# Expert blocks of 256 rows in place of 384, and the second weight split once by GpSimd during plain attention

## The reference

```python
x = x + attention_1(layernorm(x))          # 16 heads, relative positions clipped at 64
# second layer
h = layernorm(x)
q, k, v = split(h @ w_qkv + b_qkv)         # 16 heads of 16
x = x + attention(q, k, v) @ w_o + b_o     # plain attention
h = layernorm(x)
logits = h @ gate_w + gate_b
topv, topi = top_k(logits, 2)              # 2 of 8 experts per token
ew = scatter of softmax(topv)
hid = relu(h @ W1[e] + b1[e])              # 256 -> 1024
x = x + sum over the 2 experts of ew * (hid @ W2[e] + b2[e])   # 1024 -> 256
```

## Time and profile before

| | |
|---|---|
| median of 3 runs | 4359.0 us (4358.93 to 4363.57) |
| span of the profiled execution, first to last instruction | 4340.7 us, 18.3 below that median |
| mean granted clock of TensorE over the span | 0.951 of full speed |
| busy over the span: TensorE, VectorE, ScalarE, GpSimd | 91%, 80%, 69%, 33% |
| DMA: bytes, mean rate | 556 MB, 128 GB/s |

### The profile page before, as it was taken

One profiled execution on the slowest core, in us unless ns is written; L12 is line 12 of the kernel. 1 busy time (PEld: TensorE's weight loads), 2 busy tenths in 40 slices (PEclk: granted clock), 3 DMA queues, 4 the chain that ended last, 5 costly groups with the idle time before them and its releaser, 6 DMA issues. The chain is left out here.

```text
span 4340.7 us, 77253 instructions
## 1 busy us (share of the span) xinstructions
PE 3962.5 (91%) x26592; PEld 2108.1 (49%) x26592; DVE 3486.0 (80%) x6304; ACT 2981.4 (69%) x5821; POOL 1446.1 (33%) x1405
## 2 busy tenths in 40 slices
PE   8699999999999999996799999999999996599997
PEld 5355555555455555544433333333333333499997
DVE  6788888888888888835688898888888872477775
ACT  4078888888788878881148888888888883266664
POOL 0356666666666666641100000000000001522232
PEclk9599999999999999998879999999999997699998
DMA  8566666666676667635652323223323303676664
GB/s 312 152 160 171 165 171 165 170 165 170 159 172 165 170 160 172 164 81 188 201 99 31 53 38 47 44 40 46 50 36 48 43 7 89 172 218 172 170 179 110
DMA packets 486195, 556.39 MB, mean 128 GB/s; under 512 B 60260, under 2 KB 426836, under 8 KB 476524
## 3 DMA queue, kind: packets, MB, share of 16 engines
q1 hardware_dynamic: 465980, 526.94, 49.1%
q0 software_dynamic: 19824, 24.52, 3.4%
HBM read 347.67 MB, written 206.76 MB: 128 GB/s over the span
## 5 line engine op out<-in xcount | busy, mean ns | idle before, releaser
L371 DVE TENSOR_REDUCE pa_pm<-pa_psA 128x2 f32<-128x1024 f32 x1024 | 1207.9, 1219 | 134.9 <-PE pa_psA L460 134.8
L1098 ACT ACTIVATE ra_p<-ra_psS 128x512 f32<-128x512 f32 x2048 | 1082.0, 606 | 315.1 <-PE ra_psS L1175 223.8
L434 ACT ACTIVATE pa_p<-pa_psS 128x512 f32<-128x512 f32 x2048 | 1063.5, 604 | 247.4 <-PE pa_psS L486 243.1
L1009 DVE TENSOR_REDUCE ra_pm<-ra_psA 128x1 f32<-128x896 f32 x1024 | 1112.7, 1087 | 147.6 <-PE ra_psA L1133 132.7
L486 PE MATMUL pa_psS<-pa_qs,pa_zs 50*128 50x512 f32 x2048 | 793.2, 464 | 77.6 <-ACT pa_p L434 64.2
L460 PE MATMUL pa_psA<-pa_zs,pa_qs 48*128 48x512 f32 x2048 | 796.7, 472 | 38.0 <-DMA pa_zs<-k_halves 17.8
L1133 PE MATMUL ra_psA<-ra_zs,ra_qs 48*128 48x512 f32 x2048 | 729.9, 450 | 19.1 <-DVE ra_pm L1011 8.4
L1175 PE MATMUL ra_psS<-ra_qs,ra_zs 50*128 50x512 f32 (+3 forms) x2176 | 699.6, 406 | 28.4 <-ACT ra_p L1098 17.9
L486 PEld LDWEIGHTS pa_psS<-pa_qs,pa_zs 50*128 50x128 f32 x2048 | 342.2, 185 | 626.0 <-ACT pa_p L434 607.0
L1206 PE MATMUL ra_psO<-ra_p,ra_vs 128*32 128x512 f32 (+3 forms) x6400 | 551.0, 449 | 0.0
L1175 PEld LDWEIGHTS ra_psS<-ra_qs,ra_zs 50*128 50x128 f32 x2176 | 350.4, 186 | 409.0 <-ACT ra_p L1098 318.4
(11 more groups left out here) (247 smaller groups left out, 4947.2 us busy)
## 6 DMA issues: line engine op xcount, KB each, us to landing
relative_rows<-ra_rst SPq DMA_DIRECT2D x128, 512.0 KB, 3.9
ra_blk<-window_rows SPq DMA_DIRECT2D x128, 512.0 KB
mo_w_raw<-ffn_W SPq DMA_DIRECT2D x58, 1024.0 KB, 5.4
ra_zs<-k_halves SPq DMA_DIRECT2D x192, 248.0 KB, 7.1
ra_dl<-relative_rows SPq DMA_DIRECT2D x128, 256.0 KB, 4.7
window_rows<-ra_pc SPq DMA_DIRECT2D x128, 256.0 KB
pa_qs<-q_halves SPq DMA_DIRECT2D x192, 128.0 KB, 6.2
pa_zs<-k_halves SPq DMA_DIRECT2D x192, 128.0 KB, 6.8
```

Source lines behind the costliest of these rows:

```text
L371: dve.reduce_max(pm[:, par, 2 * a:2 * a + 2], psA[w][:, :, :], AX.X).then_inc(s_am.h, 1)
L434: act.activation(pr[:, i % NPR, :], psS[:, slot(i), :], ACT.Exp).then_inc(s_ex.h, 1)
L1009: dve.reduce_max(pm[:, q, i, 2 * left:2 * left + 1], psA[w][:, lo:lo + 2 * G - P], AX.X).then_inc(s_far.h, 1)
L1098: act.activation(dst, psS[:, slot(i), :], ACT.Exp if kind == "E" else ACT.Copy).then_inc(s_cp.h, 1)
```

## The change

1. `BT` is 256 in place of 384: 39 blocks in place of 29, 2 row tiles in place of 3, and all sizes that follow from it (block table, padding stores, buffers of a block).
2. In plain attention, each head t also handles one thirty-second of the second weight: SyncE loads two feature tiles (`load_w2`, 256 KB), GpSimd writes the high part and the low part (`split_w2`), and SyncE stores both to a new HBM tensor (`store_w2`, 512 KB).
3. In the expert stage the raw second weight, its casts and its subtractions go. Both parts are loaded, 2 MB in one DMA, into a ring of three, behind the wait for `second` of three blocks before.
4. The high part of the first weight is all VectorE's; its pieces are spread over f=7 of the block before the one before, f=0, 1 and 2. `turned` is split over f=2 and 3, `yb` over f=5 and 6.
5. psY is double, so `second` waits for the finish of the block before last. `finish(b-1)` goes from f=0 to f=3, `split_h(b+1)` from f=3 to f=4. `pick` and its waits are unchanged and it stays at f=5.

The core of the diff (declarations, buffers and removed helpers are left out):

```diff
+            def load_w2(t):
+                e, f = t * WQ // FC, t * WQ % FC
+                sp.dma_start(wr[:, :, :], w2_raw[e, f * P:(f + WQ) * P, :].rearrange("(f p) d -> p f d", p=P)
+                             ).then_inc(s_wl.h, 16)
+
+            def store_w2(t):
+                e, f = t * WQ // FC, t * WQ % FC
+                s_ww.wait(sp, t + 1)
+                sp.dma_start(w2_parts[e, :, :, f:f + WQ, :], wp[:, :, :, :].bitcast(F32)).then_inc(s_ws.h, 16)
...
                     if t + 1 < HEADS:
                         send_m(t + 1, p + 1)
+                    store_w2(t)
+                    if t + 1 < HEADS:
+                        load_w2(t + 1)
                     if p == 0:
                         store_o(t, it)
...
+            def split_w2(t):
+                s_wl.wait(pool, 16 * (t + 1))
+                s_ws.wait(pool, 16 * t)
+                pool.tensor_copy(wp[:, 0, :, :], wr[:, :, :]).then_inc(s_wh.h, 1)
+                s_wh.wait(pool, t + 1)
+                pool.tensor_tensor(out=wp[:, 1, :, :], in0=wr[:, :, :], in1=wp[:, 0, :, :], op=ALU.subtract
+                                   ).then_inc(s_ww.h, 1)
...
                     if U * it + p + 1 < HEADS:
                         lay_v(U * it + p + 1, p + 1)
+                    split_w2(U * it + p)
...
-BT = 384
+BT = 256
...
-                if b >= 2:
-                    sp.wait_ge(s_2l, 2 * (b - 1))
-                sp.dma_start(r2[:, b % 2, :, :], A["ffn_W2"][bass.ds(ex, 1), :, :].rearrange(
-                    "e (f p) d -> p (e f) d", p=P)).then_inc(s_r2[b % 2], 16)
+                if b >= NW2:
+                    sp.wait_ge(s_s, FC * (b - NW2 + 1))
+                sp.dma_start(w2[:, b % NW2, :, :, :].bitcast(F32), w2_parts[bass.ds(ex, 1), :, :, :, :].rearrange(
+                    "e p x f d -> p (e x) f d")).then_inc(s_w2[b % NW2], 16)
...
                 for j in range(BJ):
-                    if f == 0 and b >= 1:
-                        pe.wait_ge(s_y, BJ * (b - 1) + j + 1)
+                    if f == 0 and b >= 2:
+                        pe.wait_ge(s_y, BJ * (b - 2) + j + 1)
...
-                if f == 0 and b >= 1:
+                if b + 1 < NBLK:
+                    if u == 0:
+                        high_w1(1, 0)
+                    if f == 0:
+                        low_w1(b + 1, 0)
+                    if f == 1:
+                        high_w1(b + 1, 1)
+                    if f == 2:
+                        low_w1(b + 1, 1)
+                if f == 3 and b >= 1:
                     finish(b - 1)
                 if b + 1 < NBLK:
-                    if f == 1:
-                        high_w1(b + 1)
-                        low_w1(b + 1, 0)
-                    if f == 2:
-                        low_w1(b + 1, 1)
-                    if f == 3:
+                    if f == 4:
                         split_h(b + 1)
-                    if f == 4:
-                        high_w2(b + 1, 0)
-                        low_w2(b + 1, 0)
                     if f == 5:
-                        high_w2(b + 1, 1)
                         pick(b + 1)
-                    if f == 6:
-                        low_w2(b + 1, 1)
+                if f == 7 and b + 2 < NBLK:
+                    high_w1(b + 2, 0)
             finish(NBLK - 1)
```

More of the change, by code:

```diff
@@ L136 @@
 TURNS = 34
+WQ = NE * FC // HEADS
 F_STEP, M_STEP = 2, 11
@@ L2240, in _, with expert_stage @@
             table()
-def expert_stage(nc, A, xs, acc, out, ident, gain, b1_t, onehot, tab):
+def expert_stage(nc, A, xs, w2_parts, acc, out, ident, gain, b1_t, onehot, tab):
     NU = NBLK * FC
     NHID = 4
+    NW2 = 3
     with ExitStack() as ctx:
@@ L2275, in expert_stage @@
         y = sb("y", [P, 2, BJ, D])
-        psT = ctx.enter_context(nc.psum_tensor("mo_psT", [P, CH, G], F32))
+        psT = ctx.enter_context(nc.psum_tensor("mo_psT", [P, CH, BT], F32))
         psH = ctx.enter_context(nc.psum_tensor("mo_psH", [P, 3, G], F32))
-        psY = ctx.enter_context(nc.psum_tensor("mo_psY", [P, BJ, G], F32))
+        psY = ctx.enter_context(nc.psum_tensor("mo_psY", [P, 2, BJ, G], F32))
         s_r1 = [sem(f"s_r1{i}") for i in range(2)]
-        s_r2 = [sem(f"s_r2{i}") for i in range(2)]
+        s_w2 = [sem(f"s_w2{i}") for i in range(NW2)]
         s_x = [sem(f"s_x{i}") for i in range(3)]
@@ L2362, in second @@
                 pe.wait_ge(s_lo, u + 1)
-                if f % (FC // 2) == 0:
-                    pe.wait_ge(s_2l, 2 * b + 1 + f // (FC // 2))
+                if f == 0:
+                    pe.wait_ge(s_w2[b % NW2], 16 * (b // NW2 + 1))
                 for j in range(BJ):
-                    if f == 0 and b >= 1:
-                        pe.wait_ge(s_y, BJ * (b - 1) + j + 1)
+                    if f == 0 and b >= 2:
+                        pe.wait_ge(s_y, BJ * (b - 2) + j + 1)
                     for m, (x, z) in enumerate(PARTS):
-                        last = pe.matmul(psY[:, j, 0:D], hid[:, x, u % NHID, j * P:(j + 1) * P],
-                                         w2[:, q, z, f, :], start=f == 0 and m == 0,
+                        last = pe.matmul(psY[:, q, j, 0:D], hid[:, x, u % NHID, j * P:(j + 1) * P],
+                                         w2[:, b % NW2, z, f, :], start=f == 0 and m == 0,
                                          stop=f == FC - 1 and m == len(PARTS) - 1)
@@ L2390, in turned @@
                     act.wait_ge(s_hs, b - 1)
[L2391 to L2403, removed]
+                act.activation(hb[:, q, c, :], psT[:, c, 0:BT], ACT.Identity, bias=gain[:, 1, c:c + 1],
+                               scale=gain[:, 0, c:c + 1]).then_inc(s_hT, 1)
+            for c in range(CH):
+                turned(0, c)
             for u in range(NU):
@@ L2500, in _ @@
             split_h(0)
-            high_w1(0)
+            for c in range(CH):
+                high_w1(0, c)
             for c in range(CH):
                 low_w1(0, c)
[L2504 to L2507, removed]
             for u in range(NU):
@@ L2590, in program @@
                 route_stage(nc, A, ot_rows, f_rows, acc, xs, wo, bo, ident, gate, gain, gb, b1_t, onehot, tab)
-            expert_stage(nc, A, xs, acc, out, ident, gain, b1_t, onehot, tab)
+            expert_stage(nc, A, xs, w2_parts, acc, out, ident, gain, b1_t, onehot, tab)
 def kernel(**inputs):
```

64 lines of the change are left out of this document (26 added, 38 removed).

## The result

The changed kernel takes 4627.9 us (median of 4 runs, 4618.6 to 4632.2) against 4360.9 us (4358.9 to 4363.6) in the same comparison: a ratio of 1.061, 95% interval 1.0595 to 1.0625. The forecast was 4528 with a range of 4440 to 4640, and slower at 0.92. The cause is the forecast one; its size was put 100 us too low.

A forecast was written before the change was run, and what follows sets the result against it. TensorE bounded the expert stage at 507.5 us; with the stall, 37 blocks of 17.8 us and 2 of 11.8 make 682, 175 more. Less 6 at the edges: 4359 + 169 = 4528 us, range 4440 to 4640.

The forecast's parts named there:

- part 1: Expert stage matmuls: 11.8 us of TensorE per block, 39 blocks 460 us against 507.5 if TensorE stayed the bound.
- Part 2: Expert stage, other engines' work per block: VectorE 8.7 us, ScalarE about 8.2, both below TensorE's 11.8.
- Part 3, the mechanism: Expert stage: pick waits for block b-1's scatters, VectorE stands about 5 us, TensorE idles 4.5; block 16.3 us at full clock.
- Part 3, the landing: Expert stage: second scatter lands 4.3 us after issue, finish to landing 7.8 us; block between -0.6 and +1.3 of the figure.
- Part 3, the clock: Expert stage: TensorE's clock falls in every block for 3.4 us, costing 1.5 us, at most 1.7.
- Part 5: Plain attention: GpSimd's splits, 2.1 us per head, cost 0; ends no gain and 67 us.
- Part 4: Expert stage loads: 3.82 MB per block, 10.4 to 13.7 us with full engines, hidden under 17.8.
- Part 6: Edges: padding stores 3.6 us less, block tables 0.8 more, last block 2.2 less, stage's start about -1; sum -6 us.
- A: Rival: same stall in the expert stage, but the clock doesn't fall; block 16.3 us, 4472 us; chance 0.20.
- B: Rival: same stall, lower clock through all seven groups; block 21.3 us, 4657, with late landing 4705; B or later landings 0.14.
- C: Rival: the wait in pick is over before VectorE gets there; TensorE bounds at 11.8 us, 4306 us; chance 0.07.
- D: Rival: no stall, but the expert stage's loads bind at 13.7 us per block; 4380 us; chance 0.04.

The follow-up runs named there:

- Experiment 5: Changed kernel with SyncE issuing block b's 2 MB second-weight load only after block b-3's scatters have landed; 4499.9 us against 4342.3, ratio 1.036.
- experiment 3: Changed kernel with 22 unused matmuls of 512 columns filling TensorE's pause ahead of second(6), wait in pick kept; 4560.6 us, ratio 1.049.
- the second weight alone with the wait: Changed kernel with BT = 384, single psY and finish at f=0, wait in pick kept; ratio 1.021 to the kernel before.

## Why the prediction was right or wrong

- **The bound, part 1: right.** 11.8 us of TensorE per block is what the version without the wait takes (11.81).
- **Part 2: right.** VectorE is busy 9.04 us of a block for 8.7 forecast, ScalarE 8.16 for 8.2.
- **Part 3, the mechanism: right, step by step.** The loop's terms in the block shown, predicted and measured: finish to the second scatter's issue 3.47 and 3.34; pick to the subtraction 0.69 and 0.68; its hand-over 0.45 and 0.47; transposes to hb 0.64 and 0.64; to relu 0.46 and 0.46; to the subtraction 0.90 and 0.86; to finish 0.34 and 0.35. All the small terms hold to 0.13 us. VectorE stood before pick 37 times, as said, for 262 us in all: 7.1 us each, where about 5 were forecast; TensorE's pause was 6.4 us in the median for 4.5.
- **Part 3, the landing: the failed term.** 4.3 us was taken, "because the large loads of a block are issued when unit 7 ends, 7 us before the next finish, and are mostly through"; the median is 6.4 for a block's second scatter, and the finish-to-pick time 9.9 instead of 7.8. The "7 us" is wrong by the prediction's own chain: from unit 7's end to finish there are four groups and the small terms, 4 x 0.71 + 0.64 + 0.46 + 0.90 + 0.34 = 5.2 us. The 2 MB load is issued 5.5 us before finish in the block shown (4113.11, 4118.65) and 4.9 in the median, the first weight's behind it (4116.87), and up to the landing the DMA engines are at 0.74. Experiment 5 shows the place of the load to be the cause. The Trainium skill (DMA: Bandwidth & Descriptors, section "Issuing engines are not separate DMA queues") says that DMAs of SyncE and GpSimd run on the same 16 engines and interleave; the prediction set this aside in favour of the row, and the landings of 6.8 us with the load ahead and 3.9 without agree with it. The late end that the prediction gave, 1.3 us more, was still too small: 2.1.
- **Part 3, the clock: the second term mis-sized.** A fall in every block came, as the row of the middle stage said. It was put at 3.4 us long and 1.5 us of cost; the lower level lasted 6.8 us in 31 of 32 steady blocks, 5.66 us of it behind the pause in the block shown, and cost 1.8 us in the median (experiment 3), 2.7 in the block shown. The Trainium skill (TensorE: Matmul & The Clock Gate, section "Why this matters for your kernels") warns of pauses between bursts of matmuls for this reason. The pauses of 5.3 to 7.5 us in the changed kernel and of 3.4 to 4.4 us in experiment 5 agree: each has half clock behind it. Shorter pauses had it in some blocks: 1.8 to 2.5 us in the five of experiment 3, 2.7 to 2.9 us in four of 22 blocks of the second weight alone with the wait.
- **The sum:** the block was forecast at 16.3 + 1.5 = 17.8 us. The distance from finish to pick took 9.9 instead of 7.8, 2.1 more, and the clock 1.8 instead of 1.5, 0.3 more: 20.2, of the measured 20.36. Over 37 blocks the 2.56 us between forecast and measurement are 95 of the 100 missing microseconds.
- **Part 5: right.** Plain attention is 1 us shorter, inside its own spread; the splits took 56 us of GpSimd's time for 67 forecast.
- **Part 4: right where it was used,** since the loads did not bind; without the stall they run at 0.98 in blocks of 11.81 us, by which full engines would need some 11.6 us (an estimate), inside "10.4 to 13.7 us".
- **Part 6: -4.8 for -6.** The stage's start gained the second weight's splits and lost 4.3 us to VectorE's wait for the second block's first weight, as said.
- **Rivals.** A did not come: the clock fell. B's place was right (later landing and a longer fall) and the result lies between the forecast and B. C, the wait over before VectorE gets there, did not come; with the wait edited away its figure, 53 us less than the kernel before, is near the 51 measured (4346.0 to 4295.1). D stays out: no engine waits for a weight's DMA in the steady stage.

## What to carry to other kernels

A wait that costs nothing is hidden by a distance in the program's order; shrinking the blocks and moving its two ends closer uses that distance up, so list every wait between the moved steps and price it from issue to landing. An accumulating scatter's landing is not a constant: it depends on what was issued shortly ahead of it on the same DMA engines (3.9 to 9.5 us here), so issue large prefetches behind it, or give the buffer it protects one more slot, which here cost 16 bytes in each partition and was worth 311 us.

## What the runs showed of the hardware that was not expected

- The same scatter of 128 rows of 1 KB lands 3.9 us after its issue with the 2 MB load behind it, 6.8 with that load issued some 5 us ahead of finish, 9.5 with it issued when finish starts (medians of all scatters of the steady stage).
- TensorE's pauses of 3.4 to 4.4 us (experiment 5) and of 5.3 to 7.5 us (the changed kernel) brought its clock to the lower level in every steady block, for 3.4 us in most blocks of the one and 6.8 in most of the other; kept busy for most of the pause, it stayed at 0.98.
- The DMA engines moved 323 GB/s over 100 us of the stage in blocks of 11.8 us, and the scatters' late landing did no harm there.
- Relative attention, the same code in all kernels here, took from 1851 to 1882 us from one execution to the next. Its cause stays open.
